# A fused block kernel: the second attention's first rows loaded two turns earlier, six of its score chunks made in the last turns of the stage before

## What is computed

```python
x = x + attn_block(layernorm(x))   # pre-norm, causal attention, Wo, gelu MLP 128-512-128
x = x + ffn_block(layernorm(x))    # attention without mask, Wo + bo, layernorm,
                                   # top 2 of 8 experts (gelu MLP 128-512-128), layernorm
# attention of either block
s = einsum('bhqd,bhkd->bhqk', rope(q), rope(k)) / sqrt(8)
o = einsum('bhqk,bhkd->bhqd', softmax(s), v)
```

## Time and profile before

| | |
|---|---|
| median of 3 runs | 1604.15 us (1601.58 to 1609.94) |
| the profiled execution | 1594.96 us, of which 1593.1 us are the span from the first to the last instruction |
| busy share of the span | TensorE 87%, DVE 76%, ACT 72%, POOL 30% |
| granted TensorE clock, mean | 0.939 of full speed |
| DMA | 158.26 MB, mean 99 GB/s |

### The profile page before, as it was taken

The page is one execution under the profiler, slowest core; times in us unless marked ns, Lnnn a source line. Parts: engine busy times, 40 slices in busy tenths (PEclk is TensorE's granted clock), DMA queues, the critical chain, the costliest instruction groups (busy, mean ns, idle before and its releaser), DMA issues.

```text
span 1593.1 us, 36099 instructions
## 1 busy us (share of the span) xinstructions
PE 1386.2 (87%) x13425; PEld 602.7 (38%) x13425; DVE 1215.1 (76%) x1846; ACT 1143.0 (72%) x2357; POOL 480.9 (30%) x786
## 2 busy tenths in 40 slices
PE   5669999999998899369999999999989998999840
PEld 2323343334333566112222222322322235889730
DVE  6788888888883466799999999999999952523334
ACT  7618888888888566129999998899879986434321
POOL 5413333333333566200000002100222344323455
PEclk9959999999999999659999999999999999999975
DMA  4622112121112353301333331112001405688741
GB/s 139 195 86 75 64 46 70 44 76 52 68 46 88 116 169 116 128 6 48 108 137 125 109 95 37 43 57 91 30 35 48 134 30 152 189 247 258 234 126 56
DMA packets 130256, 158.26 MB, mean 99 GB/s; under 512 B 17313, under 2 KB 103329, under 8 KB 129825
## 3 DMA queue, kind: packets, MB, share of 16 engines
q1 hardware_dynamic: 120864, 130.77, 26.2%
q0 software_dynamic: 9216, 25.18, 4.6%
HBM read 90.90 MB, written 68.96 MB: 100 GB/s over the span
## 4 chain that ended last, share of the span: by engine, by line
PE 42%; DVE 10%; DMA 4%; issue 4%; ACT 3%; POOL 3%; SPq 1%; ACTq 0%; POOLq 0%; DVEq 0%
PE bank L628 16%; PE banks L613 9%; DVE row_max L664 7%; PE banks L585 6%; PE banks L1524 3%; PE banks L1514 3%; DMA sorted_in<-v_all,slots 2%; POOL probs L1332 2%; PE banks L1416 2%; ACT o_sums L724 1%; DMA parts<-sorted_in 1%; PE banks L337 1%; DMA qk_parts<-parts 1%; ACT front L2015 1%; PE bank L1423 0%
## 5 line engine op out<-in xcount | busy, mean ns | idle before, releaser
L664 DVE TENSOR_REDUCE row_max<-banks 128x2 f32<-128x1024 f32 (+3 forms) x896 | 933.7, 1105 | 60.8 <-PE banks L585 32.9
L709 ACT ACTIVATE probs<-banks 128x512 f32<-128x512 f32 (+3 forms) x1792 | 875.7, 553 | 116.4 <-PE banks L613 93.8
L628 PE MATMUL bank<-probs,v_ones 128*32 128x256 f32 (+2 forms) x6656 | 523.2, 386 | 11.9 <-ACT o_sums L724 10.8
L585 PE MATMUL banks<-k_work,q_work 48*128 48x512 bf16 (+3 forms) x1792 | 358.4, 376 | 66.9 <-DVE row_max L664 47.8
L613 PE MATMUL banks<-q_work,k_work 51*128 51x512 bf16 (+3 forms) x1792 | 376.5, 367 | 10.9 <-ACT probs L709 9.9
L613 PEld LDWEIGHTS banks<-q_work,k_work 51*128 51x128 bf16 x1792 | 104.4, 93 | 380.0 <-ACT probs L709 344.4
L628 PEld LDWEIGHTS bank<-probs,v_ones 128*32 128x32 f32 x6656 | 133.7, 108 | 258.1 <-ACT probs L709 174.2
L750 POOL DMA_DIRECT2D heads_out<-o_sums x64 | 36.3, 567 | 470.2 <-ACT o_sums L724 470.2
L2092 ACT ACTIVATE rope<-banks,expert 128x256 f32<-128x256 f32 x184 | 72.0, 474 | 113.5 <-PE banks L1514 113.5
L770 POOL TENSOR_SCALAR_AFFINE_SELECT probs<-probs 128x256 f32<-128x256 f32 x256 | 103.6, 408 | 127.3 <-ACT probs L709 126.5
L585 PEld LDWEIGHTS banks<-k_work,q_work 48*128 48x128 bf16 x1792 | 90.2, 95 | 125.0 <-DVE row_max L664 91.2
(11 more groups left out here) (195 smaller groups left out, 1042.5 us busy)
## 6 DMA issues: line engine op xcount, KB each, us to landing
expert<-expert_rows SPq DMA_DIRECT2D x46, 578.0 KB, 4.4
qk_parts<-parts SPq DMA_DIRECT2D x64, 256.0 KB, 2.7
heads_out<-o_sums POOLq DMA_DIRECT2D x64, 256.0 KB, 3.8
sorted_in<-front SPq DMA_DIRECT2D x21, 512.0 KB, 5.9
q_work<-qk_parts SPq DMA_DIRECT2D x64, 128.0 KB
k_work<-qk_parts SPq DMA_DIRECT2D x64, 128.0 KB
parts<-sorted_in SPq DMA_DIRECT2D x46, 128.0 KB, 4.3
q_work<-qk_parts SPq DMA_DIRECT2D x64, 64.0 KB
```

The costliest lines, as they stand in the source:

```text
L585: last = pe.matmul(to[:, par, 0:width], q[r:r + M0, pair, qt * P:(qt + 1) * P], k[r:r + M0, pair, kh * G:kh * G + width], start=True, stop ...
L628: last = pe.matmul(bank[7][32 * j:32 * j + 32, c0 + c1:c0 + c1 + w], v_ones[i % QB][:, kt, j, :], prob_slots[:, (e + j) % RING, c1:c1 + w] ...
L664: dve.tensor_reduce(row_max[:, :, pair, qt, kh], self.buf_of("chunk", g, c)[:, :, 0:width], AX.X, ALU.max).then_inc(s["chunk_max"], 1)
L709: act.activation(prob_slots[:, e % RING, 0:width], self.ring_bank("exp", e)[:, 0:width], ACT.Exp, scale=SCALE).then_inc(s["exps"], 1)
```

## The change

- *SP*: the loads of head group 0's rows go to the end of turn 6 (`i == GROUPS - 2`); those of head groups 1 and 2 come behind the last turn.
- *TensorE*: two score chunks of head group 0 come at the end of its turn 8, four more at the end of turn 9. So that chunk 1 can have banks 2 and 3, the transposes and v of the last token group go to bank 7 (`bank_of`, `LAST_HALVES`).
- *DVE*: the clearing of `row_max` and two maxima come in turn 9, between `rotate` and `residual` of token group 6; four maxima in turn 10, between those of group 7.
- The second attention's own lists start at chunk 6 in place of 0 (`EARLY`). The first attention keeps all its steps (`EARLY[1]` is 0). No instruction is added or dropped.

```diff
+EARLY = {1: 0, 2: 6}
...
+        LAST_HALVES = (2 * GROUPS - 1,)
...
+            def bank_of(self, which, n):
+                return bank[WO_BANK if n in LAST_HALVES else which]
...
-                    last = pe.transpose(bank[T_BANK][:, g * P:(g + 1) * P], z[:, g, :], ident[:, :])
+                    last = pe.transpose(self.bank_of(T_BANK, n)[:, g * P:(g + 1) * P], z[:, g, :], ident[:, :])
...
-                    last = pe.matmul(bank[V_BANK][:, g * P:(g + 1) * P], hT[:, g * P:(g + 1) * P], w_v[a][:, :],
+                    last = pe.matmul(self.bank_of(V_BANK, n)[:, g * P:(g + 1) * P], hT[:, g * P:(g + 1) * P], w_v[a][:, :],
...
-                for c in range(LEAD):
-                    chunk(0, c)
+                for c in range(self.early, LEAD):
+                    self.chunk(pe, 0, c)
...
+            def clear(self, dve):
+                dve.memset(row_max[:, :, :, :, :], LOW).then_inc(maxima_cleared, 1)
+
+            def chunk_maximum(self, dve, g, c):
+                qt, pair, kh, width, _ = self.chunks[c]
+                if c == 0:
+                    if g:
+                        dve.wait_ge(self.s["maxima"], 5 * (g - 1) + 1)
+                    else:
+                        dve.wait_ge(maxima_cleared, self.a)
+                dve.wait_ge(self.s["chunk"], g * self.nc + c + 1)
+                dve.tensor_reduce(row_max[:, :, pair, qt, kh], self.buf_of("chunk", g, c)[:, :, 0:width],
+                                  AX.X, ALU.max).then_inc(self.s["chunk_max"], 1)
...
-                dve.memset(row_max[:, :, :, :, :], LOW).then_inc(maxima_cleared, 1)
-                dve.wait_ge(maxima_cleared, self.a)
-                for c in range(LEAD):
-                    chunk(0, c)
+                for c in range(self.early, LEAD):
+                    self.chunk_maximum(dve, 0, c)
...
-                if LOAD_FROM <= i - 3 < GROUPS:
-                    attend[2].load(sp, i - 3 - LOAD_FROM)
+                if i == GROUPS - 2:
+                    attend[2].load(sp, 0)
+            for i in range(1, QB):
+                attend[2].load(sp, i)
...
                     proj[2].products(pe, GROUPS + i - 2)
                     proj[2].values(pe, GROUPS + i - 2)
+                if i == GROUPS:
+                    pe.wait_ge(mid["gelu"], FC * GROUPS)
+                    attend[2].chunk(pe, 0, 0)
+                    pe.wait_ge(proj[2].s["hT"], 2 * GROUPS - 1)
+                    pe.wait_ge(proj[2].s["v_kept"], 2 * GROUPS - 1)
+                    attend[2].chunk(pe, 0, 1)
+                if i == GROUPS + 1:
+                    for c in range(2, EARLY[2]):
+                        attend[2].chunk(pe, 0, c)
...
+            attend[1].clear(dve)
             attend[1].dve(dve)
...
                 if i + 1 < GROUPS:
                     scale_heads(i + 1)
+                if i == GROUPS + 1:
+                    attend[2].clear(dve)
+                    for c in range(0, 2):
+                        attend[2].chunk_maximum(dve, 0, c)
+                if i == GROUPS + 2:
+                    for c in range(2, EARLY[2]):
+                        attend[2].chunk_maximum(dve, 0, c)
                 if 0 <= i - 3 < GROUPS:
                     proj[2].residual(dve, GROUPS + i - 3)
```

More of the change, by code:

```diff
@@ L399, in input @@
                 if a == 1:
[L400 removed]
+                    act.activation(hT[:, :], self.bank_of(T_BANK, n), ACT.Identity, scale=cols1[:, 0:1],
                                    bias=cols1[:, 1:2]).then_inc(s["hT"], 1)
                 else:
[L403 removed]
+                    act.activation(hT[:, :], self.bank_of(T_BANK, n), ACT.Copy).then_inc(s["hT"], 1)
             def high(self, act, n):
@@ L541, in sp, with free @@
                         self.store_reciprocals(sp, i // HG - 1)
+            def free(self, pe, slot):
+                if slot < CHUNK_BUFS:
+                    return
+                what, g, c = self.slots[slot - CHUNK_BUFS]
+                if what == "chunk":
+                    pe.wait_ge(self.s["chunk_max"], g * self.nc + c + 1)
+                elif what == "product":
+                    pe.wait_ge(end["xc"], HALVES * (g + 1))
+                elif what == "turn":
+                    pe.wait_ge(end["x1T"], HALVES * (g + 1))
+                elif what == "logits":
+                    pe.wait_ge(end["gate"], HALVES * (g + 1))
+                else:
+                    pe.wait_ge(end["slots"], g + 1)
@@ new lines, in chunk @@
+            def chunk(self, pe, g, c):
+                qt, pair, kh, width, masked = self.chunks[c]
+                q, k, to = q_rows[g % QB], k_rows[g % QB], self.buf_of("chunk", g, c)
+                if c == 0:
+                    pe.wait_ge(self.rows_in[g % QB], 16 * ROW_LOADS * (g // QB + 1))
+                self.free(pe, self.slot_of["chunk", g, c])
+                for par in range(2):
+                    r = par * HALF
+                    last = pe.matmul(to[:, par, 0:width], q[r:r + M0, pair, qt * P:(qt + 1) * P],
+                                     k[r:r + M0, pair, kh * G:kh * G + width], start=True, stop=not masked)
+                if masked:
+                    for half in range(2):
+                        for par in range(2):
+                            r, c0 = par * HALF, half * HALF
+                            last = pe.matmul(to[:, par, width - P + c0:width], half_ident[r:r + HALF, half, :],
+                                             later_keys[r:r + HALF, half, c0:P], start=False, stop=half == 1)
+                last.then_inc(self.s["chunk"], 1)
@@ L687, in dve @@
                         if what == "chunk" and i + ahead < NG:
-                            chunk(i + ahead, n)
+                            self.chunk_maximum(dve, i + ahead, n)
             def act(self, act, between=None):
```

49 lines of the change are left out of this document (6 added, 43 removed).

## The result

| | before | changed |
|---|---|---|
| median of the comparison | 1602.87 us (4 runs) | 1582.76 us (4 runs, 1577.55 to 1588.89) |
| profiled execution, and its span | 1594.96, 1593.1 | 1577.55, 1575.7 |
| top_max, behind the z store of group 7 | 54.2 us | 41.1 us |
| granted TensorE clock, mean | 0.939 | 0.947 |

The ratio is 0.9866, with a 95% interval of 0.983 to 0.9902: the change makes the kernel faster, as forecast, and by more. The seam (from the z store of group 7 to top_max) gained what the sum said. The difference lies elsewhere, and most of what follows is about telling the two apart.

A forecast was written before the change was run, and what follows sets the result against it. The seam was taken as bound by a chain of DMA, ACT's copy, DVE's subtraction and 32 maxima, not TensorE. 1594.96 - 12.65 = 1582.3 us profiled; 9.2 above it the median, 1591.5, range 1584 to 1601.

The forecast's parts named there:

- the sum: Seam between the attentions: six maxima (6.8 us), the clear and the rest of DVE's 10.69 us idle go; gain 12.6 us.
- The mechanism: Seam: DMA, ACT's copy, DVE's subtraction and 32 maxima bound it; without the store's delay and six maxima, top_max comes 12.65 us earlier.
- The subtraction of group 6: DVE, turn 9: it takes 1.23 us since POOL's addition has ended; if still 2.31, the cost is 1.3 us.
- TensorE's turn of group 7, 0.9 late at no cost: TensorE, turn 8: two early chunks delay group 7's turn 0.9 us, covered because DVE's rope can't start before 643.
- Rival A: SP, turns 7 and 8: early loads delay stores; price 0 to 1 us, gain 8.6 if four stores suffer; chance 0.10.
- Rival B: TensorE's 2.4 GHz grant outlives the maxima: 2.6 us more, gain 15.2, 1589 us; chance 0.07.
- the price of the slow pace: Second attention's start: three units with values took 1.98 us each at half clock in place of 1.11, 2.6 us together.
- Rival D: Start of head group 1: its rows land late and hold TensorE and DVE; slower, 1614 us; chance 0.03.
- Rival C: No measurable change: the seam's gain is given back or the medians wander; around 1600 us; chance 0.10.
- How the numbers follow: Whole kernel: profiled 1594.96 - 12.65 = 1582.3 us, plus the 9.2 between profiled execution and median, gives 1591.5.
- the clock's 3 and 2: Range 1584 to 1601: forecast's ends 1589 and 1596, widened by 3 us for clock phase and 2 for a three-run median.

The follow-up runs named there:

- the loads alone: Changed kernel with the loads at their new places but no early chunks or maxima, against the kernel before: 1590.92 us, ratio 0.995.
- One turn later: Changed kernel with head group 0's rows loaded at the end of turn 7 in place of turn 6: 1596.86 us, ratio 0.9962 to the kernel before.
- the second comparison: The changed kernel run again with no edit, against the kernel before: 1587.14 us against 1599.17, ratio 0.9924.
- in the third: The changed kernel run once more with no edit, against the kernel before: 1582.64 us against 1595.12, ratio 0.9913.
- the two repeats: The changed kernel run twice more with no edit, against the kernel before: 1587.14 us (ratio 0.9924) and 1582.64 us (ratio 0.9913).
- fillers: Changed kernel plus unread 256-column matmuls behind chunks from the third on and head group 1's first eight: 1609.53 us, ratio 1.0045; with weights held, 1614.02 us, 1.0048.
- the smaller version: Changed kernel plus unread 128-column matmuls behind head group 0's last 12 chunks and head group 1's first 8: 1586.5 us, ratio 0.9947 to the kernel before.

## Why the prediction was right in kind and off in size

*The mechanism: right.* The path was DMA, copy, subtraction, maxima; the store left the loads behind, and nothing new took its place. Forecast 12.6 us at the seam, measured 13.1 (41.1 behind the z store where 41.5 was forecast).

*The subtraction of group 6: right.* I chose 1.23 with POOL out of the way; 1.22, 1.22 and 1.22 in the three profiles of the changed kernel, and 2.31 with the loads alone.

*TensorE's turn of group 7, 0.9 late at no cost: right.* The transposes of group 7 began 2.91 us ahead of the z store in place of 3.81. The early chunk waited 0.64 for ACT and nothing on DVE waited behind it.

*Rival A, the loads in the way of turns 7 and 8: did not happen.* ACT's copy of group 5 waited for nothing. The margin was as thin as I said: of the two stores of group 4's high part the second, issued at 616.55, landed 8.9 us later, at 625.5, and the copy started at 626.23. One turn later it was not the store but the rows themselves that were late (4.41 us).

*Rival B, a clock that stays high: did not happen*, and the row that I set against it (TensorE busy 1.36 of 3.4, then half clock) was the right one. The clock came back 16.1 us behind top_max, before 16.8. I had read the price of the slow pace too high. Not three units with values took 1.98 but two, and the third 1.36 (708.21 to 710.18, 712.16 and 713.52), so it was 2.0 us and not 2.6. The same two readings in the changed kernel are 1.98 and 1.96.

*Rival D, the rows of head group 1: did not happen.* They were issued at z + 15.05 and were there.

*Rival C: the medians do wander, but not around no change.* In three comparisons the changed kernel was faster by 0.8 to 1.3%.

*The step that failed* is the last of the sum, in "How the numbers follow": "I take that distance as belonging to the runs and not to the kernel, so the median comes to 1591.5". The sum gave 1582.3 for the profiled execution, and 9.2 on top of it for the median. Measured were 1577.55 and 5.2 on top, 1582.76. Of the 8.7 us between forecast and result, 4.0 are this term: the median lay 5.2 above the profiled execution in the result, 3.2 above it in the second comparison and 2.2 below it in the third. Only 0.4 is the seam. The other 4.3 are the rest of the kernel, which I had put at no change, and which ran shorter in that one profile (2.8 up to the z store, 1.6 behind top_max). In the other two profiles of the changed kernel it did not (1540.4 and 1541.6 us without the seam, against 1538.9 and 1541.5 before). So that part was luck of the execution. The first gain, 20.1 us, exceeds the 12.0 and 12.5 of the two repeats, and that is luck at least in part. One sign of it is the clock: the four changed executions of the first comparison had 0.943 in the mean, those of the repeats 0.940 and 0.941. By the 1.45 us for 3.4 us at half clock that is worth some 3 to 4 us, an estimate. The rest of the excess stays open.

The range fell short with it: "on either side stand the clock's 3 and 2 for a median of three such runs". Both allowances came from one profile and three times. The kernel before has since had medians from 1595.1 to 1605.5, on several chips, so the 2 should have been about 5. The centre suffers from the same. I took the 1604.15 as what this kernel needs; it is a draw from the upper end of that band. From the gain of 13 and the median of the five medians that I now have, 1602.87, the changed kernel would be put at 1590. A time by itself can't be put closer than the band; the gain against a partner in the same comparison can, and it was 12.0 and 12.5 in the two comparisons with more executions, where the sum said 12.6.

## What to carry to other kernels

When a copy waits for a store, read the queue that issued the store, not the store: here eight loads in front of it made a wait of 10.7 us, and putting them behind made the same wait on another engine, so the only gain was to issue them early by their full landing time, into a stretch where nobody is waiting. With the wait gone, look for work that fits into the short waits that remain; it can be worth more than the wait that it fills. Here two maxima of 2.3 us filled a wait of 1.12 and still gained 2.1, since they moved the subtraction out from under another engine's addition. And before giving a range, ask how much the unchanged part of the program varies between executions: in the five profiles of the two kernels it varied by 7 us, more than half of this effect, and the granted clock of each execution says much of why.

## What the runs showed of the hardware that I had not expected

*Gapless work alone did not bring the clock back.* With fillers TensorE was busy for 48.2 us of 48.2 at half clock, and for 30 us of 30 in the smaller version, and the grant stayed at 1.2 GHz. With the units and their value products it was back at 2.4 GHz at 696.2 in the changed kernel, about 8 us after the first unit's exponentials (688). That suggests the kind of work and does not show it: what differs between the two kinds (matrices of 128 against 32 columns held, more and shorter matmuls) no run here separates.
The Trainium skill (TensorE: Matmul & The Clock Gate, Part 1: The HAM clock gate) ties the granted rate to how busy the engine has been; the trace agrees for the fall in the wait of 4.4 us, and does not for 48.2 busy microseconds that stayed at half rate.

*A fall of the grant has a price that repeats.* Each 3.4 us at half clock made the same step of the second attention 1.45 us longer. The step from the twelfth top_max to the thirteenth took 44.96 us with none, 46.4 to 46.5 with one in nine profiles, and 47.8 to 47.9 with two in three.

*Eight small loads hold back a large store.* The loads move 768 KB and take 13.1 to 13.4 us wherever they stand (13.3 before, 13.1 at the end of turn 7, 13.4 behind the stores); of the two stores of a high part right behind them, the second lands 8.4 to 9.0 us after its issue, against 2.7 in the middle of all such stores. In turn 6 that went unnoticed because the next copy comes later, 9.7 us after that store's issue, not because it was cheap.
The Trainium skill (DMA: Bandwidth & Descriptors, "Why a DMA increments its semaphore by 16 and not by 1") would have such a load run on two or four DMA engines; the wait of 10.76 us for a store behind eight of them would fit that, but no run shows the engines of one transfer.

*A short wait on TensorE can cost more than itself:* after 4.41 us without work the next eight products took 5.21 us in place of 3.96.
